# Two tables for the part maxima of attention, and the maximum per query taken behind the next head's first unit

## The reference, cut to what matters

```
scores = (Q @ K.T) / sqrt(16)
A = softmax(scores, axis=-1)
A_stable = 0.6 * A + 0.4 * L        # L: a fixed narrow band
out = A_stable @ V
```

## Time and profile before

| | |
|---|---|
| median of three runs | 1911.24 us |
| the profiled execution's own time | 1914.27 us |
| its span, first to last instruction | 1912.1 us |
| its mean granted clock of TensorE | 0.990 |
| maxima reductions, line 696 | 1024, from 79.7 us on |
| `neg_max` reductions, line 704 | 32, from 128.1 to 1303.2 us |

### The profile page before, as it was taken

The page is one execution under the profiler, slowest core; times in us unless marked ns, Lnnn a source line. Parts: engine busy times, 40 slices in busy tenths (PEclk is TensorE's granted clock), DMA queues, the critical chain, the costliest instruction groups (busy, mean ns, idle before and its releaser), DMA issues. The chain is left out here.

```text
span 1912.1 us, 47937 instructions
## 1 busy us (share of the span) xinstructions
PE 1842.9 (96%) x16386; PEld 888.3 (46%) x16386; DVE 1558.8 (82%) x2092; ACT 1374.5 (72%) x2471; POOL 348.4 (18%) x407
## 2 busy tenths in 40 slices
PE   7899999999999999999999999999999999999997
PEld 3442222222222222222222222222787799999997
DVE  7599999999999999999999989992266765555554
ACT  3329999999999999999999979999444422322332
POOL 1135001000100110010001000100035522223233
PEclk9999999999999999999999989999999999999999
DMA  5422212311221232123112221220125777878884
GB/s 182 142 80 61 75 53 68 88 55 53 75 82 53 59 83 69 53 69 87 54 53 75 82 54 54 65 81 24 45 97 185 294 243 226 252 259 265 289 258 116
DMA packets 105922, 217.87 MB, mean 114 GB/s; under 512 B 21976, under 2 KB 61016, under 8 KB 105312
## 3 DMA queue, kind: packets, MB, share of 16 engines
q1 hardware_dynamic: 92688, 198.93, 32.3%
q0 software_dynamic: 13152, 17.83, 4.8%
HBM read 169.23 MB, written 65.55 MB: 123 GB/s over the span
## 5 line engine op out<-in xcount | busy, mean ns | idle before, releaser
L696 DVE TENSOR_REDUCE part_max<-psum 128x1 f32<-128x1024 f32 x1024 | 1169.1, 1215 | 44.0 <-PE psum L826 39.4
L756 ACT ACTIVATE probs<-psum 128x512 f32<-128x512 f32 x2048 | 1109.6, 597 | 53.0 <-PE psum L839 22.4
L851 PE MATMUL psum<-probs,v_ones 128*32 128x256 f32 x8192 | 656.0, 392 | 15.3 <-ACT heads_sb L772 13.0
L839 PE MATMUL psum<-score_q,score_k 50*128 50x512 f16 x2048 | 632.5, 383 | 5.0 <-issue 4.8
L826 PE MATMUL psum<-max_k,max_q 48*128 48x512 f16 x2048 | 592.9, 384 | 4.7 <-DVE part_max L696 1.8
L851 PEld LDWEIGHTS psum<-probs,v_ones 128*32 128x32 f32 x8192 | 162.9, 108 | 409.7 <-issue 212.6
L839 PEld LDWEIGHTS psum<-score_q,score_k 50*128 50x128 f16 x2048 | 151.2, 94 | 416.7 <-ACT probs L756 367.9
L1261 ACT ACTIVATE x_sb<-psum,x_sb 128x512 f32<-128x512 f32 (+1 forms) x160 | 101.4, 635 | 253.7 <-PE psum L1641 248.2
L1660 PE MATMUL psum<-w,h_hi 128*128 128x256 f32 x1120 | 201.7, 279 | 0.7 <-DVE h_lo L1462 0.4
L1660 PEld LDWEIGHTS psum<-w,h_hi 128*128 128x128 f32 x1120 | 178.3, 188 | 11.9 <-DVE h_lo L1462 1.2
L1460 DVE CAST h_hi<-x_sb 128x512 fp32r<-128x512 f32 (+1 forms) x160 | 66.0, 412 | 129.4 <-ACT x_sb L1261 129.2
(11 more groups left out here) (204 smaller groups left out, 1363.7 us busy)
## 6 DMA issues: line engine op xcount, KB each, us to landing
w<-w_split SPq DMA_DIRECT2D x40, 2048.0 KB, 8.7
xs<-in_pads SPq DMA_DIRECT2D x33, 528.0 KB, 5.2
w_split<-w_pair SPq DMA_DIRECT2D x32, 512.0 KB, 5.6
max_q<-qk_pieces SPq DMA_DIRECT2D x192, 64.0 KB, 2.2
score_k<-qk_pieces SPq DMA_DIRECT2D x192, 64.0 KB, 2.2
qk_pieces<-pieces SPq DMA_DIRECT2D x32, 256.0 KB, 2.5
w_raw<-in_we SPq DMA_DIRECT2D x32, 256.0 KB, 5.6
x_sb<-xs SPq DMA_DIRECT2D x15, 528.0 KB, 7.3
```

Source lines behind the costliest of these rows:

```text
L696: nc.vector.tensor_reduce(part_max[:, t, p:p + 1], ps_m[p].rearrange("q b f -> q (b f)"), axis=AXIS.X, op=ALU.max).then_inc(m_read, 1)
L756: nc.scalar.activation(probs[kb % 2][:, chunk * BLOCK:(chunk + 1) * BLOCK], bank_of(at), ACT.Exp, scale=by).then_inc(exp_done, 1)
L839: nc.tensor.matmul(bank_of(at), score_k[u][rows, kb * P:(kb + 1) * P], score_q[u][rows, part * BLOCK:(part + 1) * BLOCK], start=True, stop ...
L851: last = nc.tensor.matmul(ps_o[QUAD * j:QUAD * (j + 1), at:at + BLOCK // PARTS], v_ones[u][:, kb, :], probs[kb % 2][:, j * BLOCK + at:j * ...
```

## The change: what it does

`part_max` gets a second table, chosen by the parity of the head: head m writes table m % 2. `maxima` on DVE now takes one `p` at a call. `split_shift(n + 1)` reads its head's table and is called at ahead = 16, between the reduction of p = 0 and that of p = 1 of the next head's first tile; the wait for `shift_step` stands behind the reduction of p = 1. Before, the call stood behind ahead = 15, with the wait directly behind it. The other engines' text is the same.

```diff
-        def maxima(g, t):
-
-            for p in range(2):
-                dve.wait_ge(m_ready, 2 * g + p + 1)
-                nc.vector.tensor_reduce(part_max[:, t, p:p + 1], ps_m[p].rearrange("q b f -> q (b f)"),
-                                        axis=AXIS.X, op=ALU.max).then_inc(m_read, 1)
-
-        def split_shift(m):
+        def maxima(g, t, u, p):
+
+            dve.wait_ge(m_ready, 2 * g + p + 1)
+            nc.vector.tensor_reduce(part_max[:, u, t, p:p + 1], ps_m[p].rearrange("q b f -> q (b f)"),
+                                    axis=AXIS.X, op=ALU.max).then_inc(m_read, 1)
+
+        def split_shift(m, u):
 
             dve.wait_ge(m_read, 2 * ST * (m + 1))
             if not isinstance(m, int) or m > 0:
                 dve.wait_ge(shift_ready, m)
-            nc.vector.tensor_reduce(neg_max[:], part_max[:], axis=AXIS.X, op=ALU.max, negate=True
+            nc.vector.tensor_reduce(neg_max[:], part_max[:, u], axis=AXIS.X, op=ALU.max, negate=True
                                     ).then_inc(shift_step, 1)
-            dve.wait_ge(shift_step, m + 1)
...
         for t in range(ST):
-            maxima(t, t)
-        split_shift(0)
+            for p in range(2):
+                maxima(t, t, 0, p)
+        split_shift(0, 0)
...
         for t in range(LOOK - ST):
-            maxima(ST + t, t)
+            for p in range(2):
+                maxima(ST + t, t, 1, p)
 
         def body(i, last):
             for u in range(2):
                 n = 2 * i + u
                 for kb in range(ST):
                     ahead = kb + LOOK - ST
-                    if not (last and u + ahead // ST > 0):
-                        maxima(ST * (n + 1) + ahead, ahead % ST)
+                    for p in range(2):
+                        if not (last and u + ahead // ST > 0):
+                            maxima(ST * (n + 1) + ahead, ahead % ST, (u + 1 + ahead // ST) % 2, p)
+                        if ahead == ST and p == 0 and not (last and u):
+                            split_shift(n + 1, 1 - u)
+                    if ahead == ST and not (last and u):
+                        dve.wait_ge(shift_step, n + 2)
                     if kb == HEADS_AT + 1:
                         invert(n)
-                    if ahead == ST - 1 and not (last and u):
-                        split_shift(n + 1)
...
-                for n, shape, dt in (("part_max", [P, ST, 2], F32), ("neg_max", [P, ST], F32),
+                for n, shape, dt in (("part_max", [P, 2, ST, 2], F32), ("neg_max", [P, ST], F32),
```

## The result

The changed kernel took 1891.27 us (median of 6 runs, 1890.86 to 1892.26) against 1910.38 us for the kernel before (6 runs, 1904.22 to 1924.21): a ratio of 0.9878 with a 95% interval of 0.985 to 0.9907, so 19 us faster by the medians where 10 were forecast (1901 us). The runs of the changed kernel also lie close together, 1.4 us against 20.

The account below looks back on a forecast made before the run. With three engines near their limit, DVE was taken to bound around `neg_max`; 0.34 us a head times 30 gives 10.2 us, off the median 1911.24, so 1901 us, range 1890 to 1912.

Parts of the forecast that it names:

- What bounds: Around `neg_max` DVE bounds and PE waits 0.48 us; from the shift's transpose on PE has gained 0.22 us on DVE's demand.
- The size of `neg_max` without waits: On DVE, `neg_max` without a wait of its own costs 0.11 us against 0.45, judged by the reciprocal's 0.16.
- The gain per head: DVE's reductions behind `neg_max` start 0.34 us earlier and PE keeps it: 37.20 us a head, 10.2 us over 30 heads.
- The late wait: The `shift_step` wait, now behind one more reduction on DVE, costs 0; were it still to show, 0.23 us a head.
- the shift chain: `neg_max` to POOL to PE's transpose, moved 1.01 us later: cover shrinks from 2.68 to 1.33 us, cost 0.
- Rivals 1 and 3: 1: `neg_max` costs 0.45 us at either place, 1911 us (chance 0.17). 3: shift late at PE's transpose, 1929 us (0.03).
- rival 2: PE's own pace takes over: `neg_max` hides wholly, 0.47 us a head, 14.1 us in all, 1897 us (chance 0.10).
- The rule that the prediction sets against itself: Trainium skill: a semaphore after each VectorE operation costs nothing extra; `neg_max` would cost as much at either place, 1911 us.
- Head 0: Its `neg_max` stands ahead of the loop, keeps its place and waits, and is not among the 30 heads that gain.
- rival 4: Something of the run: a heap of lost time, 8.1 us at one head, PE standing 4.58; on both kernels (chance 0.05).
- the gain and a run without a heap against a run with one: What faster by over 1%, under 1892 us, was said to need; chance 0.11.

Follow-up runs that it names:

- e8: Changed kernel with four more reductions of the same part maxima right ahead of `neg_max` in each head of the loop: median 1903.84 us, ratio 0.9975.
- e7: Changed kernel with the reciprocal on DVE moved from behind kb = 2 to behind kb = 13: median 1889.37 us, ratio to before 0.9876.
- its twin: The kernel before, word for word, run as a kernel of its own: median 1913.06 us, ratio 1.0031.
- e1: The kernel before with two tables of part maxima and nothing else: median 1906.73 us, ratio 0.9967.
- e4: The kernel before with the doubled wait for `shift_step` taken out once in head 0: median 1907.1 us, ratio 0.9962.
- e10: The kernel before without PE's repeated wait for `o_copied` at kb = 1: median 1904.23 us, ratio 0.9963.
- e9: Changed kernel with two more transposes of the shift on PE in each head: median 1971.75 us, ratio 1.0265.
- e3: Changed kernel, but `neg_max`'s end is waited for directly behind it, and head 0 keeps two waits: median 1900.15 us, ratio 0.9948.
- e2: Changed kernel, but `neg_max` at its old place with only the wait behind it late; head 0 keeps two waits: median 1899.37 us, ratio 0.992.
- e5: Changed kernel with the doubled wait for `shift_step` put back in head 0: median 1893.92 us, ratio 0.9928.

## Why the prediction was right or wrong

- **What bounds: right.** DVE ahead of the shift's transpose, PE behind it. e8 and e7 move DVE's work before and past that point and a head answers by 0.37 and 0.10 us, as the two limits say.
- **The size of `neg_max` without waits: nearly.** 0.11 us by the reciprocal's row, 0.09 measured. The parts that I read off the timeline (0.13 ahead, 0.14 + 0.09 behind) each went on its own, 0.145 and 0.21.
- **The gain per head: right.** 0.34 forecast, 0.366 measured, 11.0 us in 30 heads in place of 10.2. The edges of the runs say the same: 1890.66 against 1900.99 to 1901.7, 10 to 11 us.
- **The late wait and the shift chain at 0: right.** No gap behind the p = 1 reduction; 1.31 us of cover where 1.33 were forecast. Rivals 1 and 3 are out, and rival 2 with them, since the head gained 0.366 and not 0.47. The rule that the prediction sets against itself, that a semaphore between VectorE operations costs nothing extra, does not hold for these operations: the two waits made up 0.36 of the 0.45 us.
- **Head 0: a slip.** The prediction says that its `neg_max` "keeps its place and its waits". The change drops one of the two waits for `shift_step` there, which is worth 1.1 us in the profile and is not seen in the totals.
- **The step that failed** is rival 4: "Something of the run, not of the edit ... It falls on both kernels." I had the 8.1 us in hand, in rows 8 to 10, and took it for chance that a median carries along: the forecast of 1901 us takes the gain in pace off before's median and leaves its stops in. The same step sized the outcome that came: "the gain and a run without a heap against a run with one" got 0.11, as the luck of a draw, but no run of 12 of the changed kernel was long, against 68 of the 95 later runs of the kernel before. The median of before is a floor near 1901 us and the stops of most of its runs (median excess 5 to 19 us by comparison). The profiled executions bear this out: in the six at before's pace (before, its twin, e1, e4, e8, e10), with 0 to 4 stops and times of 1904.21 to 1930.52 us, the time less what heads lasted beyond their usual length comes to 1901.5 to 1906.1. The 19 us by the medians are about 11 of pace and 8 of stops no longer met.
- **Why the changed kernel is spared** stays open. PE's text is the same in both, so both stand at the edge; e9 and e10 show that a few instructions decide there. What DVE does has a say as well, since e8 changed nothing else: over 6 us above the fastest lay 0 of 12 runs of the changed kernel at 37.18 us a head and 5 of 12 of e8 at 37.55. Between them lie 3 of 12 at 37.40 (e3) and 4 of 12 at 37.33 (e2). This looks like the tempo, but the tempo is not all: e5, at the changed kernel's pace, had 2 of 11, and among kernels of 37.54 us with the same text for PE the counts go from 5 of 12 (e1) over 6 of 12 (e4) to 11 of 12 (the twin). With a dozen runs each such counts are rough, and how the tempo would do it (perhaps by when PE asks for the block behind the loop) was not tried. So the 8 us are not owed to the mechanism that the change was made for; e10 has 6 of them (1910.37 to 1904.23) by one wait.

## What to carry to other kernels

Where an engine's timeline shows a short operation between long ones, compare its gaps on both sides with the overlap of back-to-back operations: the difference is what its own two waits cost, and each goes away separately, one by letting an independent operation in front, one by a second buffer. Then ask whether that place or a later one bounds. And if the runs of a kernel scatter upwards from a sharp edge, look for a stop of PE "for nothing" where a loop turns, with a burst of instruction fetches behind it: the loop's body may be too long for what the engine keeps, and dropping a doubled wait from it can be worth over half of an edit of the pace (here 6 us against 11). Before forecasting from a median, take the fastest run as well, and price the pace from the one and the stops from the difference.

## What the runs showed of the hardware that I had not expected

- A stop at the loop's turn costs more than its 4.6 us of standing still: 8.1 us in the kernel before. The clock granted from 1122.7 to 1131 us was 0.50, the 1.2 GHz level, and the four units behind the stop took 2.11, 1.98, 1.98 and 1.98 us where 1.11 to 1.13 is usual. The first two stand in the earlier trace rows; PE's timeline goes on:

```profile
1126.86 0.60 PE L839 MATMUL psum<-score_q,score_k 50*128 50x512 f16 x1
...
1128.84 0.60 PE L839 MATMUL psum<-score_q,score_k 50*128 50x512 f16 x1
...
1130.82 1.01 PE L862 MATMUL psum<-ident_sb,heads_sb 128*128 128x128 f32 x4
```

In e9, with a stop at every turn, the granted clock was 0.95 to 0.97 over the whole loop.
- 0.08 us decide over 1.07: DVE's tensor_tensor in head 0 lasts 0.17 us when it starts 0.02 us ahead of POOL's, 1.24 us when it starts 0.05 or 0.06 us behind.
- A repeated transpose of the same operand cost PE 0.11 us in a row, not the 0.22 that a single one adds between units (units 0.44 us apart around three in e9, 0.22 around one in the changed kernel).
